# The last MLP of each batch computed inside the loop of hyperbolic attention, its tokens normalised on GpSimd

## What is computed

```python
# hyperbolic attention: q, k, v are (B, 16, 256, 8)
q_norm_sq = jnp.sum(q * q, axis=-1, keepdims=True)
k_norm_sq = jnp.sum(k * k, axis=-1)[..., None, :]
diff_sq = q_norm_sq + k_norm_sq - 2.0 * jnp.einsum('bhnd,bhmd->bhnm', q, k)
denom = jnp.maximum((1.0 - q_norm_sq) * (1.0 - k_norm_sq), 1e-06)
dist = jnp.arccosh(jnp.maximum(1.0 + 2.0 * diff_sq / denom, 1.0))
attn = jax.nn.softmax(-dist, axis=-1)
out = einsum('bhnm,bhmd->bhnd', attn, v)  ...  @ wo.T
# MLP
h = jax.nn.relu(x @ w1 + b1)
return h @ w2 + b2
# each block
x = x + block(_layernorm(x))
```

## Time and profile before

| | us |
|---|---|
| median of 3 runs | 2563.0 (2562.39 to 2565.41) |
| span of the profiled execution | 2563.6 |
| PE busy in it | 2079.1 (81%) |
| DVE busy | 1998.1 (78%) |
| ACT busy | 1854.7 (72%) |
| POOL busy | 1663.5 (65%) |

### The profile page before, as it was taken

The page is one execution under the profiler, slowest core; times in us unless marked ns, Lnnn a source line. Parts: engine busy times, 40 slices in busy tenths (PEclk is TensorE's granted clock), DMA queues, the critical chain, the costliest instruction groups (busy, mean ns, idle before and its releaser), DMA issues. The chain is left out here.

```text
span 2563.6 us, 50172 instructions
## 1 busy us (share of the span) xinstructions
PE 2079.1 (81%) x14935; PEld 1515.9 (59%) x14935; DVE 1998.1 (78%) x6007; ACT 1854.7 (72%) x3188; POOL 1663.5 (65%) x1516
## 2 busy tenths in 40 slices
PE   4999999999999979999947666666666666666599
PEld 4777777777777668888834444443433444434266
DVE  4677777777777757877768999999999999999522
ACT  2666666666666634344239999999999999999743
POOL 2767766676667400000058999999999999999600
PEclk7999999999999969999966677777777777777599
DMA  5000000000000024334200000000000000000011
GB/s 136 1 2 2 1 1 0 1 0 1 1 0 1 2 67 108 93 92 110 68 1 1 1 1 0 0 0 0 0 0 0 0 0 0 0 0 1 7 31 37
DMA packets 44067, 49.03 MB, mean 19 GB/s; under 512 B 5112, under 2 KB 27038, under 8 KB 43934
## 3 DMA queue, kind: packets, MB, share of 16 engines
q1 hardware_dynamic: 35614, 43.32, 7.0%
q10 hardware_dynamic: 8320, 4.19, 0.7%
HBM read 42.78 MB, written 4.72 MB: 19 GB/s over the span
## 5 line engine op out<-in xcount | busy, mean ns | idle before, releaser
L1460 POOL TENSOR_TENSOR u<-u,spare 128x1024 f32<-128x1024 f32 x256 | 597.2, 2372 | 35.1 <-ACT spare L1433 34.9
L545 ACT ACTIVATE prob<-s_ps,nmax 128x128 f32<-128x128 f32 (+1 forms) x1024 | 364.4, 432 | 140.1 <-DVE nmax L602 140.0
L1353 PE MATMUL d_ps<-rowsT 28*128 28x256 f32 x1024 | 165.9, 404 | 331.3 <-DVE u L1532 331.2
L602 DVE CUSTOM_DVE_ANT_0 s_ps<-s_ps,mask 128x128 f32<-128x128 f32 (+1 forms) x1024 | 341.3, 385 | 101.8 <-issue 77.9
L1353 PEld LDWEIGHTS d_ps<-rowsT 28*128 28x128 f32 x1024 | 106.2, 242 | 430.4 <-issue 430.0
L582 POOL TENSOR_TENSOR g_lo<-g_all,g_hi 128x512 fp32r<-128x512 f32 x256 | 329.1, 1286 | 21.4
L1528 DVE TENSOR_SCALAR u<-d_ps 128x1024 f32<-128x1024 f32 x256 | 311.9, 1218 | 39.5 <-PE i_ps L1353 39.3
L1532 DVE SCALAR_TENSOR_TENSOR u<-i_ps,u 128x1024 f32<-128x1024 f32 x256 | 313.5, 1225 | 14.8
L1471 POOL TENSOR_TENSOR spare<-spare,u 128x1024 f32<-128x1024 f32 x128 | 303.1, 2368 | 10.7
L1447 ACT ACTIVATE u<-u 128x1024 f32<-128x1024 f32 x256 | 258.3, 1070 | 0.0
L1450 ACT ACTIVATE u<-u 128x1024 f32<-128x1024 f32 x256 | 257.5, 1066 | 0.0
(11 more groups left out here) (265 smaller groups left out, 5577.9 us busy)
## 6 DMA issues: line engine op xcount, KB each, us to landing
w_all<-w_rows SPq DMA_DIRECT2D x128, 256.0 KB, 5.6
x<-L_attn_x ACTq DMA_DIRECT2D x8, 512.0 KB, 14.0
y<-y_rows SPq DMA_DIRECT2D x16, 256.0 KB, 2.3
wkqv<-L_attn_Wkqv SPq DMA_DIRECT2D x4, 528.0 KB, 8.7
gate_rows<-L_ffn_gate_proj SPq DMA_DIRECT2D x1, 512.0 KB, 14.5
up_rows<-L_ffn_up_proj SPq DMA_DIRECT2D x1, 512.0 KB, 11.5
down_cols<-L_ffn_down_proj SPq DMA_DIRECT2D x1, 512.0 KB, 13.3
w_rows<-wT SPq DMA_DIRECT2D x8, 64.0 KB, 1.6
```

What stands on the lines that cost most here:

```text
L545: last = nc.scalar.activation(prob[:, kind, at, :].rearrange("p c n -> p (c n)"), s_ps[kind][:, at.start * P:at.stop * P], ACT.Exp, bias=n ...
L602: last = nc.vector.tensor_tensor_reduce(out=scores, in0=scores, in1=keep.mask[:, N - width:N], scale=-1.0, scalar=3.4e38, op0=ALU.add, op1 ...
L1353: last = nc.tensor.matmul(ps[:, e * W2 + j * N:e * W2 + (j + 1) * N], rowsT[at, slot(i, p), 1, j * P:(j + 1) * P], rowsT[at, slot(i, p), 0 ...
L1460: nc.gpsimd.tensor_tensor(u[:, slot(i, p), :], u[:, slot(i, p), :], spare[:, p % SPARE, :], ALU.add).then_inc(sum_done, 1)
```

## The change

`mlp` and the `rstd_of_all` ahead of it are gone. The MLP of a batch runs in the attention's loop, spread over the iterations behind the one that finishes the batch's attention:

- iteration b+3: VectorE takes the moments (p = 3 and 4), ScalarE their root (`act_std4`, 128x2, ahead of the roots), VectorE 1/std (`dve_rstd4`, p = 6), GpSimd normalises the two tiles (`pool_norm4`, two instructions of 127 columns behind the sum of p = 5)
- iteration b+4: TensorE turns them into the second half of `misc` right behind `pe_turn_x` (p = 0), ScalarE copies both halves in one instruction of 512 columns (`act_both_xT`), TensorE multiplies with w1 in two halves into `r_ps[0]` and `r_ps[1]` (`pe_hidden`, at p = 2 and 3, ahead of the products with V), ScalarE takes the two ReLUs behind its second `act_hi`, and at the end of p = 7 TensorE multiplies with w2 (`pe_y`, with b2 as a product of a row of ones) into the half of `o_ps` that VectorE has copied
- iteration b+5: VectorE adds it to x (`dve_y`, p = 0), SyncE stores the batch.

b1 goes into w1: the last column of the normalised tokens is 1, and w1's last row is replaced by b1 (`pe_fold_w1`, `act_fold_w1`, once). GpSimd's code is written out over all 32 batches, that of the other engines for the first six. Behind the loop stand the MLPs of the last four batches, between the last steps of attention.

```diff
+        def pe_turn_x4(pe, b, i, to, into):
+            pe.wait_ge(xh4_done, (b + 1) * TB)
+            for j in range(TB):
+                last = nc.tensor.transpose(to[:, into + j * P:into + (j + 1) * P], xh4[:, i, j, :], keep.ident)
+            last.then_inc(x4_turned, 1)
+        def pe_hidden(pe, b, half, rows_read):
...
+            pe.wait_ge(rowsT_done[half], rows_read)
+            after(pe, relu_done, 2 * b - 1 + half)
+            for n in range(HW):
+                w = half * HW + n
+                last = nc.tensor.matmul(r_ps[half][:, n * N:(n + 1) * N], w1[:, w * P:(w + 1) * P], xTs[:, 1, :], start=True,
+                                        stop=True)
+        def pe_y(pe, b, copies):
+            pe.wait_ge(o_copied, copies)
+            pe.wait_ge(relu_done, 2 * (b + 1))
+            after(pe, y_done, b)
+            for j in range(TB):
+                out = o_ps[:, N + j * P:N + (j + 1) * P]
+                nc.tensor.matmul(out, ones_row[:, :], keep.biases[0:1, R_B2:R_B2 + P], start=(j == 0), stop=False,
+                                 skip_group_check=True)
+                for w in range(WB):
+                    last = nc.tensor.matmul(out, hidden[:, w, j * P:(j + 1) * P], w2[:, w, :], start=False,
...
+        def act_both_xT(act, b, b4):
+            act.wait_ge(xh_turned, b + 1)
+            act.wait_ge(x4_turned, b4 + 1)
+            after(act, qkv_ready, b * TB)
+            after(act, h_ready, 2 * b4)
+            nc.scalar.copy(xTs[:, :, :].rearrange("p s n -> p (s n)"), misc[:, :]).then_inc(xT_done, 1)
...
+        def pool_norm4(pool, b, i):
+            pool.wait_ge(rstd4_done, b + 1)
+            after(pool, x4_turned, b - TURN + 1)
+            for j in range(TB):
+                nc.gpsimd.tensor_scalar(xh4[:, i, j, 0:P - 1], keep.x[:, b * TB + j, 0:P - 1], part_mv[:, i, j, 0:1],
+                                        rstd4[:, i, j:j + 1], ALU.subtract, ALU.mult).then_inc(xh4_done, 1)
...
+                            pe_turn_x4(pe, b - 4, (i - 4) % TURN, misc, N)
...
+                            pe_hidden(pe, b - 4, HIDDEN_AT.index(p), (b + 1) * (HP // 2))
...
+                            pe_y(pe, b - 4, 2 * b)
...
+                    if three_before:
+                        act_std4(act, b - 3, i)
...
+                        if p == NORM4_AT and three_before:
+                            pool_norm4(pool, b - 3, i)
```

More of the change, by code:

```diff
@@ L1364, in pe_values @@
                 after(pe, o_copied, b * 2 + g // 2)
+            if g == 0:
+                after(pe, y_done, b - 3)
             for j in range(TB):
@@ L1574, in turn, with written_out @@
                     known = isinstance(b, int)
-                    body(b, i, not known or b >= 1, not known or b >= 2, not known or b >= 3, not known or b + 1 < batches,
-                         not known or b + 2 < batches)
+                    before = lambda n: not known or b >= n
+                    behind = lambda n: not known or b + n < batches
+                    body(b, i, before(1), before(2), before(3), before(4), before(5), behind(1), behind(2))
             whole = batches // TURN
-            turn(0, TURN)
-            with engine.Fori(1, whole) as r:
+            for r in range(2):
+                turn(r, TURN)
+            with engine.Fori(2, whole) as r:
                 turn(r, TURN)
             turn(whole, batches % TURN)
+        def written_out(body):
+            for b in range(batches):
+                body(b, b % TURN, b >= 1, b >= 2, b >= 3, b >= 4, b >= 5, b + 1 < batches, b + 2 < batches)
         END = batches - 1
@@ L1661, in body @@
                             act_hi(act, b + 1, p // 2)
+                        if four_before and p == 2:
+                            for half in range(2):
+                                act_relu(act, b - 4, half)
                         if two_after and p == 4:
                             act_norm(act, b + 2)
+                    if three_before:
+                        act_std4(act, b - 3, i)
                     for p in range(HP):
@@ new lines, in _, with dve_moments @@
+                last = lambda b: b % TURN
+                def dve_moments(b):
+                    dve.wait_ge(res_done, b + 1)
+                    dve_stats(b, last(b))
+                    dve.wait_ge(stats_done, (b + 1) * TB)
+                    dve_aggregate(b, last(b))
+                dve_y(dve, END - 4)
+                dve_residual(dve, END - 2)
+                dve_moments(END - 2)
+                for j in range(TB):
+                    dve_normalise(dve, END - 1, j)
+                dve_residual(dve, END - 1)
@@ new lines, in _ @@
+                dve_moments(END - 1)
+                dve_y(dve, END - 3)
+                for n in range(2):
+                    dve_copy_o(dve, END, n, last(END))
+                for b in (END - 2, END - 1):
+                    dve_rstd4(dve, b, last(b))
+                for j in range(TB):
+                    dve_normalise(dve, END, j)
+                dve_residual(dve, END)
+                dve_moments(END)
+                dve_y(dve, END - 2)
+                dve_rstd4(dve, END, last(END))
```

335 lines of the change are left out of this document (164 added, 171 removed).

## The result

The changed kernel takes 2663.7 us (median of 4 runs, 2651.4 to 2669.8), 1.0375 times the kernel before (2564.2 in its runs beside it; 95% interval 1.0355 to 1.0396). About one of these 3.75 per cent comes from stalls of TensorE ahead of the loop, which the changed kernel had here and the kernel before had not; they are not bound to the change, as the last experiments show. The prediction was 2548 with a range of 2530 to 2590: wrong, and on the side of the loss. The profiled execution has a span of 2649.6 us, 86.0 more than the 2563.6 of before and 101.4 more than the 2548.2 of the forecast.

What follows compares the result with a forecast made beforehand. TensorE bounds the MLP, ScalarE is busiest in attention. Batches grow 3.25 us to 37.39 (+87.8); with +0.7, +4.5, +2.6, +3.1 and -114.1 at the tail, -15.4 gives span 2548.2, predicted 2548 us, range 2530 to 2590.

Steps and rivals of the forecast that it cites:

- the price of the normalisation: GpSimd's two 127-column instructions per batch: 0.56 us together, ends 0.38 and 2.1 us.
- the third rival: GpSimd's instruction with scalars from memory costs as much as a 1020-column one: +1.5 us a batch, 2588 us; chance 0.10.
- I expect half speed only at the head and take 0.4: ScalarE's waits for TensorE behind the turn of the tokens: 0.4 us a batch, bounds 0 and 3.4.
- The second loop: VectorE and TensorE, pairs to pairs, with the w2 products ahead: 36.3 us a batch, 38.3 with those at half clock.
- the first loop: Closed loop ScalarE, GpSimd's sums and normalisation, TensorE's turn, ScalarE: 37.39 us a batch.
- The first three: Rivals: TensorE half clock behind the turn (0.13); w2 products at half clock, VectorE-TensorE loop longer (0.12); dear GpSimd normalisation (0.10).
- The last step before the final roots: Last first root to final roots, without head copies: from 29.7 to 34.2 us, +4.5.
- where the new wait is: ScalarE stands 2.35 us a batch before the xT copy, waiting for tokens normalised behind GpSimd's sixth sum, then turned.
- ScalarE's added work: Wider xT copy, two ReLUs and a small root in each batch: together 1.3 us.
- folding w1: Two 512-column products behind the first pairs, once: +0.7 us, between 0 and 3.4.
- the end: Batch 31 to the end, with the MLP stage replaced by the last batches' MLPs: -108.4 us.
- the fourth rival: The turn of the tokens is not late, ScalarE alone bounds: about 35.0 us a batch, 2483 us; chance 0.07.

Runs made afterwards that it cites:

- the last experiments: Kernel before and changed kernel, each unchanged and profiled once more: spans 2591.1 and 2646.1 us, both with the stalls ahead of the loop.
- e3: Changed kernel with the w2 products and VectorE's addition moved to p=4: 2630.1 us, 1.0241 times the kernel before.
- e4: Changed kernel with GpSimd's normalisation behind the fourth sum instead of the sixth: 2628.6 us, 1.0228 times the kernel before.
- e13: Changed kernel with normalisation behind the fourth sum, w2 products late and three quarters of the w2 contraction left out: 2576 us.
- e14: Changed kernel with w2 products at p=4 and only the first of each batch's two token tiles normalised: 2585 us.
- e5: Changed kernel with w2 products and VectorE's addition at p=4 and normalisation behind the fourth sum: 2515.1 us, 0.9742 times the kernel before.
- e6: e5 with the b1 rows turned by TensorE in the first stage, as in the kernel before: 2513.0 us, 0.9743 times the kernel before.
- e12: e6 plus six 256-column TensorE products that nobody reads, in TensorE's longest idle time of a batch: 2526 us.
- e7: e6 with the normalisation behind the fifth sum instead of the fourth: 2568.3 us, 0.9928 times the kernel before.

## Why the prediction was wrong, point by point

**What failed first is the price of the normalisation** ("on the line between them 127 columns cost 0.32 for one, and 0.56 for two"): 1.61 us. The line through a 4-column and a 1020-column instruction did not hold, although the prediction had said that the form was not in the trace. +1.05 a batch, some 28 us of the 77. Nearly the third rival, which had 1.5 and a chance of 0.10.

**"I expect half speed only at the head and take 0.4".** Half clock cost 0.8 a batch more than that (39.21 of e3 less 38.44), some 21 us: in e3 the way from the xT copy to the next first root is 20.72 us in a quick batch and 22.56 in a slow one, so 0.9 in the mean for the 0.4, and the rest is mostly the turn itself at half clock. The w1 products, too, were reckoned at 1.7 and 3.4 us and take 2.1 and 4.0 there. The reason given was that after 3.40 us of unbroken work the clock had stood at 1.00. In the slow batch of the changed kernel it did not; stretches of its timeline:

```profile
1812.00:1818.00 6.00, 2.86 (x32) 1.68 (x28) 5.23 (x15) 5.97 (x8) 0.55 (x1) 0.55 0.00 0
1818.00:1824.00 6.00, 5.79 (x39) 3.65 (x31) 4.79 (x8) 6.00 (x8) 5.22 (x3) 0.50 0.00 0
1824.00:1828.80 4.80, 4.57 (x25) 3.65 (x25) 4.77 (x6) 4.80 (x6) 4.80 (x3) 0.50 0.00 0
1828.80:1834.20 5.40, 5.40 (x21) 4.54 (x20) 0.28 (x1) 2.82 (x4) 5.40 (x4) 0.50 0.00 0
1834.20:1836.40 2.20, 2.20 (x16) 1.94 (x16) 1.92 (x3) 0.16 (x1) 2.20 (x2) 0.50 0.20 60
```

TensorE was busy 18.0 of 18.4 us from 1818.0 on, and at half clock throughout. One pattern of one batch was read as a rule. The Trainium skill, TensorE: Matmul & The Clock Gate, Part 4, says that a transpose does not count as TensorE being busy in the same way, which the prediction set aside; the fourth stretch is w2 products alone, without a transpose, and at 0.50 as well, so that this rule by itself does not account for it.

**The second loop** ("36.3 us, and 38.3 if y runs at half clock"): 39.14 alone (e4). The w2 products were taken as 2.2 us at full clock and 4.5 at half; they last 3.2 (1986.02 to 1989.26 in e4) and 5.45. The four bias products, of one row, were counted as passes like the others, at 0.112 each; they take 0.8 us at full clock and 1.4 at half, where 0.45 was reckoned. The 16 others take 0.136 each at full clock (1.09 for eight), not 0.112. e13 confirms the place: with fewer passes the batch falls by 1.6.

**"At 37.4 the first loop is the longer by a microsecond"**: the two are as long as each other (39.21 and 39.14), and together longer than either, 40.18, since now one and now the other is late: 1.0 a batch more, some 26 us. This is the least certain part of the sum, for the same loop had 39.34 to 40.62 in five profiles.

**The rivals as alternatives.** The first three were priced at 2588, 2572 and 2588 us, each over the forecast alone. All three occurred at once. Their excesses summed, 40 + 24 + 40, give 2652, and the range held only one at a time. That this sum is near the 2663.7 is luck: in the loop the three came to 77 us and not 104, and the stalls, which none of them has, made up most of the rest.

**The end of the range** took no account of the stalls: 21.5 us, which the profile of before did not have. With them in both kernels the spans are 2649.6 and 2591.1, a ratio of 1.023. The last step before the final roots was also misread: it took 30.7 us before (2358.42 to 2389.12) and not 29.7, and takes 37.7 now.

**Right:** where the new wait is, and that it is a closed loop without slack (e14: 0.81 out, 0.81 gained); ScalarE's added work; folding w1 (+0.6 for +0.7); the end (-105.5 for -108.4); ScalarE as the bound at about 35.0 once nothing is late, which the fourth rival gave: e5 has 35.22, and the profiled execution of e6, which has no stalls, a span of 2485.5 for its 2483; that closeness is in part luck, since its batches are 0.35 longer and its head and end shorter than reckoned.

## What to carry to other kernels

Where work is put into a stage with two closed loops, price both with their own dearest rows, and let unlikely prices that can occur together occur together in the range. A loop to which the forecast leaves one microsecond to spare is best treated as having none. A step on a closed loop costs by its place: the same instructions, moved to where their input was long there, turned a loss of 2.3% into a gain of 3.1% (profiled spans of after, e5 and before, all with five stalls). And an instruction whose form the trace does not show is better priced at the nearest dear row than on a line through cheap ones.

## What the runs showed of the hardware

GpSimd took 0.81 us for 127 columns with two scalars per partition from memory, where a 1020-column instruction with constants takes 1.06. No run has this form at another width, so how much of it depends on the columns stays open. TensorE's clock stayed at half for over 15 us while it was busy nearly all the time (above, and e12), and the same instructions took 671.51 or 788.26 us of it in e14 and e7; removing 0.8 us of GpSimd's work took away 20 us of slow batches. One execution of a program can move instruction packets at each pass of a hardware loop and another none: 97 packets for 52, with five idle stretches of 3.5 us, 27.5 us in all.
